# Two of sixteen states turned by TensorE and scaled by ScalarE, two of six products dt·x by VectorE, in a Mamba layer's scan

## What is computed

```python
dt = softplus(einsum('blr,dr->bld', dt, dt_w) + dt_b)
A = -exp(A_log)
def step(h, inp):
    dt_t, B_t, C_t, x_t = inp
    dA = exp(dt_t[:, :, None] * A[None])
    dBx = (dt_t * x_t)[:, :, None] * B_t[:, None, :]
    h = dA * h + dBx
    y_t = einsum('bdn,bn->bd', h, C_t)
    return (h, y_t)
y = ys + xc * D
y = y * silu(z)
out = einsum('bld,cd->blc', y, out_proj_w)
```

## Time and profile before

| | |
|---|---|
| three runs | 6802.38, 6807.70, 6810.25 us, median 6807.7 |
| the profiled execution | 6805.57 us, its span 6803.8 us |
| scan stage, attention layer | 0 to 5479 us, 5479 us to the end |
| busy over the span | PE 87%, PEld 55%, DVE 90%, ACT 69%, POOL 79% |
| mean granted TensorE clock | 0.933 |

### The profile page before, as it was taken

How to read it: one execution, slowest core, us unless ns; L and a number is a source line. 1 busy time by engine, 2 the same in 40 slices (tenths; PEclk the granted TensorE clock), 3 DMA queues, 4 the chain that set the end, 5 groups by cost and what they waited for, 6 DMA issues and landing times. The chain is left out here.

```text
span 6803.8 us, 98814 instructions
## 1 busy us (share of the span) xinstructions
PE 5952.4 (87%) x32764; PEld 3750.3 (55%) x32764; DVE 6135.0 (90%) x7732; ACT 4676.5 (69%) x8698; POOL 5349.5 (79%) x4332
## 2 busy tenths in 40 slices
PE   7888888888888888888888888888888769999998
PEld 3555555555555555555555555555555447777776
DVE  6999999999999999999999999999999956666665
ACT  3777777777777777777777777777777633333332
POOL 2999999999999999999999999999999931001010
PEclk8999999999999999999999999999999779999999
DMA  6222222222222222222222222222222212222221
GB/s 260 101 101 103 102 105 101 101 103 101 101 101 101 103 101 101 101 102 108 103 101 101 103 102 101 101 101 103 107 101 101 86 62 72 87 72 83 76 77 65
DMA packets 175206, 681.54 MB, mean 100 GB/s; under 512 B 28045, under 2 KB 28269, under 8 KB 141669
## 3 DMA queue, kind: packets, MB, share of 16 engines
...
## 5 line engine op out<-in xcount | busy, mean ns | idle before, releaser
L862 POOL TENSOR_TENSOR dbx<-u,bb 128x512 f32<-128x512 f32 x3072 | 3827.6, 1278 | 37.7 <-DVE p_da L706 18.4
L706 DVE TENSOR_TENSOR_SCAN p_da<-p_da,state_v,dbx 128x512 f32<-128x512 f32 x2112 | 2620.9, 1273 | 53.1 <-ACT p_da L567 52.9
L567 ACT ACTIVATE p_da<-dt,neg_a 128x512 f32<-128x512 f32 x3072 | 2073.3, 687 | 85.0 <-DVE h L713 9.6
L989 PEld LDWEIGHTS p_yt<-ident,hc_v 128*128 128x128 f32 x8448 | 1116.4, 153 | 1157.9 <-issue 824.6
L989 PE MATMUL p_yt<-ident,hc_v 128*128 128x128 f32 x8448 | 1394.3, 295 | 196.4 <-DVE hc_v L722 196.0
L722 DVE TENSOR_TENSOR hc_v<-cc,p_da 128x512 f32<-128x512 f32 x2112 | 1391.4, 666 | 0.0
L871 POOL TENSOR_TENSOR hc_g<-h,cc 128x512 f32<-128x512 f32 x960 | 1225.3, 1276 | 109.6 <-DVE h L713 109.6
L713 DVE TENSOR_TENSOR_SCAN h<-p_da,state_g,dbx 128x512 f32<-128x512 f32 x960 | 1218.2, 1269 | 60.6 <-issue 31.8
L927 PE MATMUL p_g<-xs,win 128*128 128x512 f32 x2304 | 1173.3, 604 | 73.3 <-ACT zt L519 36.0
L573 ACT ACTIVATE state_v<-p_da 128x1 f32<-128x1 f32 x2112 | 351.2, 166 | 958.8 <-DVE hc_v L722 947.0
L1425 POOL TENSOR_TENSOR x_low<-axn,x_upper 128x512 fp32r<-128x512 f32 x96 | 127.3, 1355 | 1046.2 <-DVE x_upper L1377 1046.2
...
## 6 DMA issues: line engine op xcount, KB each, us to landing
bb<-bc_spill SPq DMA_DIRECT2D x128, 1024.0 KB, 10.6
cc<-bc_spill SPq DMA_DIRECT2D x128, 1024.0 KB, 10.0
...
xj<-xc_spill SPq DMA_DIRECT2D x192, 256.0 KB, 4.1
zj<-z_spill SPq DMA_DIRECT2D x192, 256.0 KB, 2.7
...
```

The source lines that it names most:

```text
L567: nc.scalar.activation(p_da[n % RD][:], dt[:, d % 2, :], ACT.Exp, scale=neg_a[:, d, n:n + 1])\
L706: nc.vector.tensor_tensor_scan(psum, psum, dbx[:, n % RB, :], state_v[:, d, k:k + 1], ALU.mult, ALU.add).then_inc(s_scan, 1)
L862: nc.gpsimd.tensor_tensor(dbx[:, n % RB, :], u[:, d % 2, :], bb[:, n, :], ALU.mult)\
L989: last = nc.tensor.matmul(p_yt[d % 2][:, b * P:(b + 1) * P], product[:, b * P:(b + 1) * P], ident[:], start=False, stop=n == NS - 1, is_tr ...
```

## The change

- States 7 and 11 (BY_TURN) leave DVE's product. DVE scans them into h in SBUF (RH from 5 to 7). PE's `turn_state` (slots 9 and 12) transposes h into the idle bank p_yt[(d+1) % 2]. There positions are the partitions, so that C of a state is one column a block: ACT's `times_ct` (slots 10 and 15) copies the four 128x128 blocks to hct with that column as scale, and PE transposes them back behind `turn_back` of the next tile, into the same sum. `turn_c` and `copy_ct` make the columns of C once a chunk.
- BY_POOL changes from (0, 3, 6, 9, 12) to (0, 3, 6, 9, 14); DVE is left with 9 products a tile. The last columns of all seven states in h are kept by one reduce in slot 14.
- u of tiles 2 and 4 is made by DVE, in slot 11 of the tile before; the other four by POOL, in slot 14 instead of 15.
- cc holds 14 states. RV goes from 5 to 3, LAG_V from 2 to 1, LAG_G from 3 to 1. POOL's product of state 14 falls into slot 1 of the next tile. Most slots of the side jobs move.

```diff
--- before.py
+++ after.py
@@ -41,24 +41,30 @@
 NQ = DIM // P
 
 TAPS = HALO + 1
-BY_POOL = (0, 3, 6, 9, 12)
-BY_DVE = tuple(n for n in range(NS) if n not in BY_POOL)
-NDV, NPL = len(BY_DVE), len(BY_POOL)
-
-RB, RH, RD = 4, 5, 4
-RV, RG = 5, 3
-LAG, LAG_V, LAG_G = 3, 2, 3
+BY_POOL = (0, 3, 6, 9, 14)
+BY_TURN = (7, 11)
+BY_DVE = tuple(n for n in range(NS) if n not in BY_POOL + BY_TURN)
+BY_H = tuple(sorted(BY_POOL + BY_TURN))
+BY_C = tuple(n for n in range(NS) if n not in BY_TURN)
+NDV, NPL, NTN, NHS = len(BY_DVE), len(BY_POOL), len(BY_TURN), len(BY_H)
+LAST_ADDED = max(BY_DVE + BY_POOL)
+
+RB, RH, RD = 4, NHS, 4
+RV, RG = 3, 3
+TURN_STATE_AT, TIMES_CT_AT, KEEP_AT = (9, 12), (10, 15), 14
+LAG, LAG_V, LAG_G = 3, 1, 1
 OUT_BANK = (1, 1, 0)
 
-MEAN_AT, CENTRE_AT, SQUARE_AT = 2, (3, 7, 9), (7, 8, 9)
-VAR_AT, RSTD_AT, NORM_AT = 12, 11, (15, 16, 17)
-OUT_AT, OUT_SLOTS, RESIDUAL_AT = (9, 15, 19), (3, 1, 1), (14, 20, 23)
-IN_AT, IN_SLOTS = (20, 39, 57), (18, 18, 19)
-COPY_LATER, SILU_LATER = 2, (4, 2, 3)
-X_AT, COPY_X_AT, SCALE_AT = (80, 82, 83), 83, (87, 90, 92)
-
-COPY_Y_AT, TURN_AT, GATE_AT = 3, 4, 6
-DT_AT, SOFTPLUS_AT, SKIP_AT, DT_X_AT = 6, 6, 8, 15
+MEAN_AT, CENTRE_AT, SQUARE_AT = 1, (3, 9, 11), (6, 8, 9)
+VAR_AT, RSTD_AT, NORM_AT = 11, 11, (16, 17, 18)
+OUT_AT, OUT_SLOTS, RESIDUAL_AT = (7, 13, 19), (1, 4, 2), (12, 18, 24)
+IN_AT, IN_SLOTS = (22, 41, 59), (18, 18, 19)
+COPY_LATER, SILU_LATER = 1, (8, 4, 2)
+X_AT, COPY_X_AT, TURN_C_AT, COPY_CT_AT, SCALE_AT = (79, 80, 81), 82, 86, 91, (89, 90, 94)
+
+COPY_Y_AT, TURN_AT, GATE_AT = 1, 4, 6
+DT_AT, SOFTPLUS_AT, SKIP_AT, DT_X_AT = 7, 7, 12, 14
+U_BY_DVE, U_AT = (2, 4), 11
 
 
 def out_at(j, t):
@@ -242,13 +248,15 @@
         zj = sb("zj", [P, CH])
 
         bb = sb("bb", [P, NS, CH])
-        cc = sb("cc", [P, NS, CH])
+        cc = sb("cc", [P, len(BY_C), CH])
         dbx = sb("dbx", [P, RB, CH])
         h = sb("h", [P, RH, CH])
         hc_v = sb("hc_v", [P, RV, CH])
         hc_g = sb("hc_g", [P, RG, CH])
         state_v = sb("state_v", [P, ND, NDV])
-        state_g = sb("state_g", [P, ND, NPL])
+        state_h = sb("state_h", [P, ND, NHS])
+        ct = sb("ct", [P, 2, NT, NS])
+        hct = sb("hct", [P, NTN, NT, P])
         yt_s = sb("yt_s", [P, CH])
         yg = sb("yg", [P, ND, CH])
 
...
@@ -384,14 +407,16 @@
                 sp.dma_start(bb[:, 4 * k:4 * k + 4, :], src).then_inc(s_bl[k], 16)
 
             def load_c(q, k):
-                src = bc_d[q, NS + 4 * k:NS + 4 * k + 4, :].rearrange("(o n) t -> o n t", o=1).to_broadcast([P, 4, CH])
-                sp.dma_start(cc[:, 4 * k:4 * k + 4, :], src).then_inc(s_cl[k], 16)
+                these = [n for n in BY_C if n // 4 == k]
+                at, count = BY_C.index(these[0]), len(these)
+                src = bc_d[q, NS + these[0]:NS + these[0] + count, :].rearrange("(o n) t -> o n t", o=1)
+                sp.dma_start(cc[:, at:at + count, :], src.to_broadcast([P, count, CH])).then_inc(s_cl[k], 16)
 
             def load_xj(i, d):
 
                 m = i * ND + d
                 sp.wait_ge(s_dx, m + C_ONE)
-                sp.wait_ge(s_u, m + C_ONE)
+                u_done(sp, m - 1)
                 if d % 2 == 0:
                     sp.wait_ge(s_xcs[d // 2], i * 16 + 16)
                 sp.dma_start(xj[:], xc_d[i, :, d, :]).then_inc(s_xjl, 16)
...
@@ -571,6 +597,25 @@
                 m, k = i * ND + d, BY_DVE.index(n)
                 act.wait_ge(s_hcv, m * NDV + k + 1 + C_HCV)
                 nc.scalar.activation(state_v[:, d, k:k + 1], p_da[n % RD][:, CH - 1:CH], ACT.Copy).then_inc(s_stv, 1)
+
+            def copy_ct(q):
+                act.wait_ge(s_ctm, q + 1)
+                if q > 1:
+                    act.wait_ge(s_ht, (q - 1) * (ND * NTN) + NTN)
+                turned = p_g[1][:, 0:NT * 64].rearrange("p (b c) -> p b c", c=64)
+                nc.scalar.activation(ct[:, q % 2], turned[:, :, 32 + NS:64], ACT.Copy).then_inc(s_ct, 1)
+
+            def times_ct(i, d, n):
+                m, k = i * ND + d, BY_TURN.index(n)
+                act.wait_ge(s_tm, m * NTN + k + 1)
+                if k == 0:
+                    act.wait_ge(s_yb, m + 1 + C_ONE)
+                if d == 0 and k == 0:
+                    act.wait_ge(s_ct, i + 1)
+                for b in range(NT):
+                    last = nc.scalar.activation(hct[:, k, b, :], p_yt[(d + 1) % 2][:, b * P:(b + 1) * P], ACT.Copy,
+                                                scale=ct[:, i % 2, b, n:n + 1])
+                last.then_inc(s_ht, 1)
 
 
             def affine(part):
...
@@ -694,6 +744,13 @@
                 dve.wait_ge(s_res, i * NJ + j + 1 + C_RES)
                 nc.vector.bn_stats(stats[:, (i * NJ + j) * 6:(i * NJ + j) * 6 + 6], back[:, j, :]).then_inc(s_stat, 1)
 
+            def dt_x(i, d):
+                m, r = i * ND + d, d % 2
+                dve.wait_ge(s_dt, m + 1)
+                dve.wait_ge(s_xjl, m * 16 + 16)
+                dve.wait_ge(s_dbx, m * NS)
+                nc.vector.tensor_tensor(u[:, r, :], dt[:, r, :], xj[:], ALU.mult).then_inc(s_uv, 1)
+
             def scan(i, d, n):
                 m, e = i * ND + d, (i * ND + d) * NS + n
                 psum = p_da[n % RD][:]
@@ -707,10 +764,13 @@
                                                  ALU.mult, ALU.add).then_inc(s_scan, 1)
                 else:
 
-                    k = BY_POOL.index(n)
-                    dve.wait_ge(s_hcg, m * NPL + k + 1)
-                    dve.wait_ge(s_stg, m * (NPL // RH) + k // RH + C_ONE)
-                    nc.vector.tensor_tensor_scan(h[:, k % RH, :], psum, dbx[:, n % RB, :], state_g[:, d, k:k + 1],
+                    k = BY_H.index(n)
+                    if n in BY_POOL:
+                        dve.wait_ge(s_hcg, m * NPL + BY_POOL.index(n) + 1)
+                    elif m:
+                        dve.wait_ge(s_tm, (m - 1) * NTN + BY_TURN.index(n) + 1)
+                    dve.wait_ge(s_stg, m + C_ONE)
+                    nc.vector.tensor_tensor_scan(h[:, k, :], psum, dbx[:, n % RB, :], state_h[:, d, k:k + 1],
                                                  ALU.mult, ALU.add).then_inc(s_scan, 1)
 
             def times_c(i, d, n):
@@ -719,15 +779,13 @@
                 dve.wait_ge(s_hvf, m * NDV + k + 1)
                 if d == 0 and n == min(k for k in BY_DVE if k // 4 == n // 4):
                     dve.wait_ge(s_cl[n // 4], i * 16 + 16)
-                nc.vector.tensor_tensor(hc_v[:, (m * NDV + k) % RV, :], cc[:, n, :], p_da[n % RD][:], ALU.mult)\
+                nc.vector.tensor_tensor(hc_v[:, (m * NDV + k) % RV, :], cc[:, BY_C.index(n), :], p_da[n % RD][:], ALU.mult)\
                     .then_inc(s_hcv, 1)
 
-            def keep_state(i, d, k):
-
-                n = BY_POOL[k * RH + RH - 1]
-                dve.wait_ge(s_scan, (i * ND + d) * NS + n + 1 + C_SCAN)
-                nc.vector.tensor_reduce(state_g[:, d, k * RH:(k + 1) * RH], h[:, :, CH - 1:CH], AX.X, ALU.max)\
-                    .then_inc(s_stg, 1)
+            def keep_states(i, d):
+
+                dve.wait_ge(s_scan, (i * ND + d) * NS + BY_H[-1] + 1 + C_SCAN)
+                nc.vector.tensor_reduce(state_h[:, d, :], h[:, :, CH - 1:CH], AX.X, ALU.max).then_inc(s_stg, 1)
 
 
             def input_stats(c):
...
@@ -812,8 +870,10 @@
                             times_c(i, d, n - 1)
                         if n == NS - 1 and n in BY_DVE:
                             times_c(i, d, n)
-                        if n in BY_POOL and BY_POOL.index(n) % RH == RH - 1:
-                            keep_state(i, d, BY_POOL.index(n) // RH)
+                        if n == KEEP_AT:
+                            keep_states(i, d)
+                        if n == U_AT and d + 1 in U_BY_DVE:
+                            dt_x(i, d + 1)
                         if i == 0 and d * NS + n == AFFINE_AT[0]:
                             affine_means(1)
                         if i == 0 and d * NS + n == AFFINE_AT[2]:
...
@@ -883,10 +942,15 @@
 
                         if n >= LAG and n - LAG in BY_POOL:
                             times_c(i, d, n - LAG)
-                        if n == DT_X_AT and (d < ND - 1 or i + 1 < NCH):
+                        if n < LAG and i + d > 0 and n - LAG + NS in BY_POOL:
+                            times_c(*((i, d - 1) if d > 0 else (i - 1, ND - 1)), n - LAG + NS)
+                        if n == DT_X_AT and (d + 1) % ND not in U_BY_DVE and (d < ND - 1 or i + 1 < NCH):
                             dt_x(*((i, d + 1) if d < ND - 1 else (i + 1, 0)))
 
             chunks(pool, body)
+            for n in range(NS - LAG, NS):
+                if n in BY_POOL:
+                    times_c(NCH - 1, ND - 1, n)
 
 
         @block.tensor
...
@@ -997,8 +1062,37 @@
                 pe.wait_ge(s_yts, m + 1 + C_ONE)
                 for b in range(NT):
                     last = nc.tensor.matmul(p_yt[(d + 1) % 2][:, b * P:(b + 1) * P], yt_s[:, b * P:(b + 1) * P],
```

(38 more changed lines are left out.)

43 lines of the change are left out of this document (30 added, 13 removed).

## The result

The changed kernel takes 6860.3 us (median of six runs, 6855.05 to 6862.94), the one before 6806.2 beside it: a ratio of 1.0079 with a 95% interval of 1.0066 to 1.0092. It is 54 us slower, where 104 us faster was forecast, and lies 70 us above the range. The profiled execution took 6855.05 us, its span 6853.0.

A forecast was written before the change was run, and what follows sets the result against it. DVE bounds the chunk into tile 1, then POOL. 166.87 − 163.2 − 0.4 = 3.3 us a chunk, 31 of them 102 us, last chunk 1.6; 6805.6 − 104 = 6702 us, range 6640 to 6790.

The forecast's parts named there:

- a chain over the chunk: Scan stage: DVE's time up to POOL's last wait plus POOL's operations behind it; 163.2 us a chunk after the change.
- I take 0.6 for the wait: DVE's u in slot 11 of tiles 1 and 3: waits 0.6 us each, half a POOL operation.
- Both bounds: Beside u, from x_upper in the attention layer: DVE waits 0 to 1.25 us, POOL loses 0 to 0.68.
- The new placement of the twelve extras changes little: DVE, tiles 0 and 1: moved normalisation, residual and statistics operations all stay ahead of g = 26, the 26th scan counted from 0.
- at nothing: PE's added transposes, 130 us becoming 136 of 163 a chunk, hidden by its idle time; priced at no cost.
- forecast 0.4 us a chunk: ACT in tiles 2 to 5: lateness from SiLU blocks and times_ct, beyond POOL's lead, costs 0.4 us a chunk.
- The rival in which ACT gives part back: Tiles 2 to 5: ACT's idle time can't shrink enough; chunk 164.9 to 167.8 us, about 6770 us; chance 0.22.
- the slower one, ACT standing for `turn_state`: Tiles 2 to 5: times_ct waits for PE, delaying decays; gain gone at 0.8 us a block, 6850 at 1; chance 0.13.
- POOL's loss, 0.45: POOL loses 0.45 us beside each u of DVE: observed 0.2 plus 0.25 for u's greater length.
- u does nothing: Rival: POOL loses 1.24 us beside u for the 1.24 spared; 2.5 a chunk gained, 6727 us; no separate chance.
- POOL alone: Rival: DVE's excess in tiles 0 and 1 fits POOL's lead; chunk 161.8 us, 6642 us; chance 0.10.
- its first candidate: POOL's last wait at g = 25 (tile 1, state 9): 46.6 us of DVE, then 92 POOL operations and two losses, 161.6.

The follow-up runs named there:

- the one wide activation: Changed kernel with all u made by POOL and each times_ct one 512-column activation instead of four of 128: 6743.2 us, against 6742.9 with four.
- The probes: Kernel before plus test blocks behind its attention layer, DVE operations among unbroken POOL products; two-SBUF-input product at eight phases: 1.06 to 1.66 us.

## Why the prediction was wrong

Its reading of the kernel before, DVE to the end of tile 1, POOL from there, a chain over the chunk, is not contradicted by any run. The sum failed at two terms.

- **u, the step "I take 0.6 for the wait".** DVE stands 1.54 − 0.67 = 0.9 us in tile 1 and 3.89 − 0.67 = 3.2 in tile 3, 4.1 us a chunk instead of 1.2. Both bounds came from x_upper, and "the rest of a POOL operation" was taken for the most that can be. In the trace of the kernel before this is so: each of the 36 x_upper that met a POOL operation got in at its first end. In tile 3 u let two ends pass. Tile 3 is in POOL's half of the chain, so the forecast priced only what POOL loses beside u there, 0.45. But DVE that stands for longer than POOL's four buffers last stops POOL. Such a stop in tile 3 (1.9 us, and 0.4 behind it) is no term of the sum. Together: 117 us lost against u by POOL, where the gain of two POOL operations a chunk was forecast. Shown are that the two SBUF inputs and POOL's work beside them make the loss; why u lets ends pass stays open.
  The Trainium skill (SBUF — State Buffer, "Who interferes with whom") has the two exclude each other, the later one blocked entirely, for as long as the other's instruction lasts. The probes agree in the order of turns (the product ends 0.55 us after a POOL operation's end, in every phase); DVE's wait past two ends, 3.2 us, is more than that rule gives, and POOL's loss, 0.45 us a product of 0.67, less.
- **"The new placement of the twelve extras changes little", and PE "at nothing".** The mean moved up a slot, the centre stayed in slot 3, and POOL's product of state 14 now ends in slot 1 or 2 of the next tile, ahead of the mean in PE's order. The forecast saw the late add and asked only if PE had time in all, at 0.43 us a 512-column instruction. It had; but the mean starts later, and with the clock partly or mostly at its lower level its six instructions take 3.07 or 4.34 us instead of 6 · 0.43 = 2.6. Behind the first chunk, in which both kernels wait, it was late by 0.6 to 2.1 us in 16 of the chunks, and in none of the kernel before. This cost 50 us.
- **ACT, right.** 0.284 us a block against 0.29; DVE's waits for decays grew from 62 to 105 us in 4000, 1.8 us a chunk of waiting. With u by POOL they are 68, and there the one wide activation moved the time by nothing (forecast 0.4 us a chunk); that POOL's lead takes them fits this and was not tested by itself. The rival in which ACT gives part back has chunks of 164.9 us and more, and with the centre later they are 163.7; the slower one, ACT standing for `turn_state`, needs 0.8 us a block, and it is 17.4 us in 4000. Both are false.
- **POOL's loss, 0.45, right** where u gets in between its operations (4.19 for 3.74), so that the 1.24 of "u does nothing" is not seen. Against "POOL alone" stands the run with an input in PSUM: without any loss beside u it would have 166.87 − 3.5 − 2.5 = 160.9 us a chunk, and it has 163.8, with POOL still waiting for DVE for 90 us in 4000.

With both losses out, u by POOL and the centre later, the kernel takes 6693 us, where 6702 was forecast. The chain of the prediction done again with u by POOL gives the same 163.2 (its first candidate, 46.6 + 94 · 1.24, is then the largest), with ACT's 0.4 163.6, and the chunks are 163.7. So the size of the gain in the rest was right; that 6702 itself is near is luck, since that kernel has its u elsewhere. For u on DVE with nothing lost beside it the same sum gives 162.55 us a chunk, 6669 us, and the run with an input in PSUM took 6699: what the 30 us are stays open, with DVE's waits for ACT (98 us in 4000) the largest of its waits there.
